# An adaptive-condition FFN on one core: the order of the first loads, who fetches the sample numbers, and how many warm-up matmuls precede the first product

## The reference, cut to what matters

```python
def reference(x, itok, weights, inter_w, inter_b, output_w, output_b):
    # x (32, 64, 1024), itok (32,) with values 0..15, weights (16, 64, 64)
    W = weights[itok]                              # one 64x64 matrix per sample
    y = einsum('bct,bcd->bdt', x, W)               # condition product
    h = gelu(einsum('bsd,df->bsf', y, inter_w) + inter_b)   # 1024 -> 4096
    out = einsum('bsf,fd->bsd', h, output_w) + output_b     # 4096 -> 1024
    return x + out
```

## Time and profile before

| | |
|---|---|
| median of 3 runs | 1261.03 us (1260.89 to 1261.08) |
| profiled execution: own time | 1260.64 us |
| its span | 1258.8 us |
| PE busy | 1253.7 us, 100% of the span |
| DVE busy | 825.6 us, 66% |
| ACT busy | 566.9 us, 45% |
| POOL busy | 188.1 us, 15% |
| granted TensorE clock | 1.0 (mean of the core) |

### The profile page before, as it was taken

The page is one execution under the profiler, slowest core; times in us unless marked ns, Lnnn a source line. Parts: engine busy times, 40 slices in busy tenths (PEclk is TensorE's granted clock), DMA queues, the critical chain, the costliest instruction groups (busy, mean ns, idle before and its releaser), DMA issues.

```text
span 1258.8 us, 15370 instructions
## 1 busy us (share of the span) xinstructions
PE 1253.7 (100%) x5664; PEld 1043.1 (83%) x5664; DVE 825.6 (66%) x1087; ACT 566.9 (45%) x969; POOL 188.1 (15%) x95
## 2 busy tenths in 40 slices
PE   9999999999999999999999999999999999999998
PEld 9888888888888888888888888888888888888887
DVE  5977787676577777657655455554547767784764
ACT  4845454454544444444434444444444444444442
POOL 4362223321000000000034233312200000000000
PEclk9999999999999999999999999999999999999999
DMA  9586655764997322349835224544189932223431
GB/s 343 160 275 244 242 196 222 283 250 177 384 392 283 97 89 99 101 165 360 310 137 195 95 119 174 184 184 145 74 330 396 351 132 93 101 101 100 155 131 51
DMA packets 94090, 249.28 MB, mean 198 GB/s; under 512 B 7328, under 2 KB 15552, under 8 KB 92608
## 3 DMA queue, kind: packets, MB, share of 16 engines
q1 hardware_dynamic: 93408, 248.14, 54.6%
q10 hardware_dynamic: 576, 0.15, 0.1%
q0 software_dynamic: 32, 0.00, 0.0%
HBM read 162.28 MB, written 85.98 MB: 197 GB/s over the span
## 4 chain that ended last, share of the span: by engine, by line
PE 97%; DVE 1%; DMA 1%; SPq 0%; POOL 0%; ACT 0%; issue 0%; ACTq 0%; DVEq 0%
PE ps L580 48%; PE ps L564 48%; DMA w_raw<-in_L_ffn_inter_w_dram 1%; PE ps L517 1%; POOL s_w L476 0%; SPq L321 0%; DVE y_whole L795 0%; DVE acc L878 0%; DVE lhs L800 0%; DVE y_whole L782 0%; DVE y L789 0%; SPq L318 0%; ACT lhs L646 0%; ACT y_stage L623 0%; SPq L317 0%
## 5 line engine op out<-in xcount | busy, mean ns | idle before, releaser
L564 PE MATMUL ps<-y,lhs 128*128 128x512 f32 x2688 | 611.4, 389 | 0.0
L580 PE MATMUL ps<-rhs,lhs 128*128 128x512 f32 x2688 | 609.6, 389 | 0.0
L580 PEld LDWEIGHTS ps<-rhs,lhs 128*128 128x128 f32 x2688 | 504.7, 188 | 104.6
L564 PEld LDWEIGHTS ps<-y,lhs 128*128 128x128 f32 x2688 | 504.2, 188 | 104.3
L716 ACT ACTIVATE lhs<-h_raw 128x512 fp32r<-128x512 f32 x224 | 141.6, 632 | 345.8 <-PE ps L580 340.2
L859 DVE TENSOR_TENSOR lhs<-h_raw,lhs 128x512 fp32r<-128x512 f32 x224 | 155.0, 692 | 188.5 <-ACT lhs L716 188.5
L800 DVE TENSOR_TENSOR lhs<-w_raw,lhs 128x512 fp32r<-128x512 f32 x128 | 111.1, 870 | 131.6 <-ACT lhs L646 131.5
L646 ACT ACTIVATE lhs<-w_raw 128x512 fp32r<-128x512 f32 x128 | 80.9, 633 | 171.7 <-PE ps L564 165.2
L862 DVE TENSOR_TENSOR rhs<-W,rhs 128x512 fp32r<-128x512 f32 x224 | 153.3, 684 | 0.0
L800 DVE TENSOR_TENSOR lhs<-s_w,lhs 128x512 fp32r<-128x512 f32 x96 | 91.3, 953 | 89.3 <-ACT lhs L646 89.1
L468 POOL TENSOR_TENSOR s_w<-w_raw 128x1024 f32<-128x1024 f32 x16 | 48.9, 3055 | 620.3 <-PE ps L580 354.0
(11 more groups left out here) (38 smaller groups left out, 290.1 us busy)
## 6 DMA issues: line engine op xcount, KB each, us to landing
h_raw<-h_mem SPq DMA_DIRECT2D x112, 512.0 KB, 3.3
w_raw<-in_L_ffn_inter_w_dram SPq DMA_DIRECT2D x32, 1024.0 KB, 8.6
h_mem<-hs SPq DMA_DIRECT2D x64, 512.0 KB, 4.5
W<-in_L_ffn_output_w_dram SPq DMA_DIRECT2D x32, 1024.0 KB, 12.4
h_mem<-c SPq DMA_DIRECT2D x48, 512.0 KB, 5.4
y_mem<-y_out SPq DMA_DIRECT2D x28, 512.0 KB, 3.5
y<-y_mem SPq DMA_DIRECT2D x7, 2048.0 KB, 12.8
acc<-in_x_dram SPq DMA_DIRECT2D x16, 512.0 KB, 9.0
```

What stands on the lines that cost most here:

```text
L564: last = nc.tensor.matmul(ps[:, bank, :], w[:, k, :], y[i][:, part, k, :], start=(i in FRESH and k == 0 and u == 0), stop=(k == KH - 1 and ...
L580: last = nc.tensor.matmul(ps[:, bank2(h, j, tb), :], lhs[s % RING][:, a, blk(tb)], rhs[r][:, w, :], start=(j in FRESH and q == 0 and u == ...
```

## The change

- SyncE: the first half of the first token tile goes ahead of the first half of the condition matrices.
- The sample numbers are loaded by ScalarE's queue, ahead of its half of the condition matrices, instead of by GpSimd's; the bias rows by GpSimd's queue instead of ScalarE's.
- Each picking engine reads its first number (`which`) after the wait for the numbers and ahead of the wait for the condition matrices.
- GpSimd makes `ident` behind its six picks; one zeroing of `wdiag` goes to VectorE; the activation that loads the Gelu table reads `ones` and waits for these.
- WARM is 9 instead of 15.

```diff
-    WARM = 15
+    WARM = 9
@@
-        def pick(engine, i):
+        def which(engine, i):
+
+            return engine.value_load(itok_sb[0:1, i:i + 1], min_val=0, max_val=SETS - 1)
+
+        def pick(i, number):
 
             j, s = divmod(i, PER)
-            which = engine.value_load(itok_sb[0:1, i:i + 1], min_val=0, max_val=SETS - 1)
             rows = slice(s * C, (s + 1) * C)
-            return wdiag[rows, j:j + 1, rows], cond_all[:, bass.ds(which, 1), :]
+            return wdiag[rows, j:j + 1, rows], cond_all[:, bass.ds(number, 1), :]
@@ SyncE
+            sp.dma_start(x0[:, 0, 0:BANK], x_tok[0, :, 0, 0:BANK]).then_inc(x0_half, 16)
             sp.dma_start(cond_all[:, 0:SETS // 2], cond_sets[:, 0:SETS // 2]).then_inc(cond_in, 16)
-            sp.dma_start(x0[:, 0, 0:BANK], x_tok[0, :, 0, 0:BANK]).then_inc(x0_half, 16)
             sp.dma_start(x0[:, 0, BANK:D], x_tok[0, :, 0, BANK:D]).then_inc(x0_in[0], 16)
@@ GpSimd
-            pool.dma_start(itok_sb[0:1], itok.rearrange("(o b) -> o b", o=1)).then_inc(itok_in, 16)
+            pool.dma_start(b1_rows[0:F // P], b1.rearrange("(a p) -> a p", p=P)).then_inc(b1_in, 16)
             nc.gpsimd.memset(wdiag[0:C, :, C:P], 0.0).then_inc(wdiag_zero, 1)
-            nc.gpsimd.memset(wdiag[C:P, :, 0:C], 0.0).then_inc(wdiag_zero, 1)
+            pool.wait_ge(itok_in, 16)
+            number = which(pool, 0)
+            pool.wait_ge(cond_in, 32)
+            for i in range(0, TILES * PER, 3):
+                to, of = pick(i, which(pool, i) if i > 0 else number)
+                nc.gpsimd.tensor_copy(to, of).then_inc(picked[0], 1)
             nc.gpsimd.memset(ident[0:F // P], 0.0).then_inc(ident_zero, 1)
...
-            pool.wait_ge(itok_in, 16)
-            pool.wait_ge(cond_in, 32)
-            for i in range(0, TILES * PER, 3):
-                to, of = pick(pool, i)
-                nc.gpsimd.tensor_copy(to, of).then_inc(picked[0], 1)
@@ ScalarE
+            act.dma_start(itok_sb[0:1], itok.rearrange("(o b) -> o b", o=1)).then_inc(itok_in, 16)
             act.dma_start(cond_all[:, SETS // 2:SETS], cond_sets[:, SETS // 2:SETS]).then_inc(cond_in, 16)
-            act.dma_start(b1_rows[0:F // P], b1.rearrange("(a p) -> a p", p=P)).then_inc(b1_in, 16)
-            act.wait_ge(ident_made, 1)
-            nc.scalar.activation(table_ahead[0:F // P, 0:1], ident[0:F // P, 0:1], ACT.Gelu_apprx_tanh)
+            act.wait_ge(ones_made, 1)
+            nc.scalar.activation(table_ahead[:, 0:1], ones[:, 0:1], ACT.Gelu_apprx_tanh)
             act.wait_ge(itok_in, 16)
+            number = which(act, 1)
             act.wait_ge(cond_in, 32)
@@ VectorE
             nc.vector.memset(ones[:], 1.0).then_inc(ones_made, 1)
+            nc.vector.memset(wdiag[C:P, :, 0:C], 0.0).then_inc(wdiag_zero, 1)
             dve.wait_ge(itok_in, 16)
+            number = which(dve, 2)
             dve.wait_ge(cond_in, 32)
```

More of the change, by code:

```diff
@@ L447, in picks1 @@
                 for i in range((TILES + first_j) * PER, (TILES + end_j) * PER):
-                    to, of = pick(pool, i)
+                    to, of = pick(i, which(pool, i))
                     nc.gpsimd.tensor_copy(to, of).then_inc(picked1, 1)
@@ L735, in y1_high @@
                 nc.scalar.activation(y1_out[item % 2][:, 0, :], y1_in[:, (0, 0, 0, 3, 1, 2, 2)[i], :], ACT.Copy).then_inc(y1_hi, 1)
+            act.dma_start(itok_sb[0:1], itok.rearrange("(o b) -> o b", o=1)).then_inc(itok_in, 16)
             act.dma_start(cond_all[:, SETS // 2:SETS], cond_sets[:, SETS // 2:SETS]).then_inc(cond_in, 16)
-            act.dma_start(b1_rows[0:F // P], b1.rearrange("(a p) -> a p", p=P)).then_inc(b1_in, 16)
-            act.wait_ge(ident_made, 1)
-            nc.scalar.activation(table_ahead[0:F // P, 0:1], ident[0:F // P, 0:1], ACT.Gelu_apprx_tanh)
+            act.wait_ge(ones_made, 1)
+            nc.scalar.activation(table_ahead[:, 0:1], ones[:, 0:1], ACT.Gelu_apprx_tanh)
             act.wait_ge(itok_in, 16)
+            number = which(act, 1)
             act.wait_ge(cond_in, 32)
             for i in range(1, TILES * PER, 3):
-                to, of = pick(act, i)
+                to, of = pick(i, which(act, i) if i > 1 else number)
                 nc.scalar.activation(to, of, ACT.Copy).then_inc(picked[1], 1)
@@ L908, in _ @@
             nc.vector.memset(ones[:], 1.0).then_inc(ones_made, 1)
+            nc.vector.memset(wdiag[C:P, :, 0:C], 0.0).then_inc(wdiag_zero, 1)
             dve.wait_ge(itok_in, 16)
+            number = which(dve, 2)
             dve.wait_ge(cond_in, 32)
             for i in range(2, TILES * PER, 3):
-                to, of = pick(dve, i)
+                to, of = pick(i, which(dve, i) if i > 2 else number)
                 nc.vector.tensor_copy(to, of).then_inc(picked[2], 1)
```

## The result

The changed kernel takes 1264.04 us, the median of 18 runs (1261.08 to 1266.40), against 1260.95 (18 runs, 1260.22 to 1262.41) of the kernel before: a ratio of 1.0024, 95% interval 1.0018 to 1.0030. It is 3.1 us slower, and its runs spread over 5.3 us instead of 2.2. The forecast was 1260.9 with a range up to 1262.3; the result lies outside it.

A forecast was written before the change was run, and what follows sets the result against it. TensorE's unbroken matmul run was taken to bound the kernel, its start set by a chain from the first weight DMA. 1261.03 with 0 for the products, -0.1 for that DMA and 0 for the rest gave 1260.9 us, range 1260.3 to 1262.3.

The forecast's parts named there:

- part 1: Start of the condition products: condition matrices there at 5.4 us, first product at about 6.15 instead of 6.55, 0.4 earlier.
- part 5: Six fewer warm-up matmuls at the front: 1.37 us less warm-up but no saving; TensorE idle about 1.15 us, clock term 0.
- rival (d): Front: condition matrices land at 6.5, products start at 7.25; TensorE 0.7 us later, 0.41 free: +0.3, 1261.3 us; chance 6%.
- the skill's ring order: Load queues: SyncE's condition half stands behind the half tile's bytes, landing nearer 6.5 than 4.6; first product no earlier.
- Part 2: Condition products at tile 1: TensorE waits for it until 8.35 us, so of 0.4 us gained 0.03 stay.
- Part 3: End of the products: covered 1.5 us by VectorE's low parts; TensorE's lateness costs nothing for its first 0.41 us.
- Part 4: First weight DMA: issued at 7.24 us again, landing moved by -0.1 us, between -0.41 and +0.2; the term that decides.
- Rival (b): TensorE's clock low for one 3.2 us stretch of the products: 1.6 us lost, 0.41 free, +1.2, 1262.2 us; chance 18%.
- Rival (c): TensorE's clock low for two such stretches, 6.4 us of the products: +2.8, 1263.8 us; chance 3%.
- Part 6: Front, remaining moves (bias rows, `ident`, zeroing, table activation, numbers' load): all covered, cost 0.

The follow-up runs named there:

- hold_tiles: The changed kernel with 15 warm-up matmuls and SyncE waiting for both condition halves ahead of tile 0's second half and everything behind it; 1263.01 us (ratio 1.0015).
- after_w15: The changed kernel with 15 warm-up matmuls instead of 9; 1262.83 us (ratio 1.0015 to the kernel before).
- both_moves: The kernel before with half tile ahead of SyncE's condition half, numbers ahead of ScalarE's, bias rows on GpSimd's queue; 15 warm-up matmuls; 1262.37 us (ratio 1.0009).
- after_w24: The changed kernel with 24 warm-up matmuls instead of 9; 1262.42 us (ratio 1.0008 to the kernel before).
- before_w9: The kernel before with 9 warm-up matmuls instead of 15, nothing else; 1261.58 us (ratio 1.0006).
- early_only: The changed kernel with all loads on the queues and in the order of the kernel before, and 15 warm-up matmuls; 1261.28 us (ratio 0.9999).
- fifteen_narrow: The kernel before with its 15 warm-up matmuls 32 columns wide instead of 128; 1263.49 us (ratio 1.0018).
- before_w25: The kernel before with 25 warm-up matmuls instead of 15; 1262.03 us (ratio 1.0007).
- best: The changed kernel with 15 warm-up matmuls, ScalarE's condition half ahead of the numbers, and the first weight half issued ahead of the last tile; 1260.78 us (ratio 0.9998).
- nine_wide: The kernel before with 9 warm-up matmuls instead of 15, the first six twice as wide (256 columns); 1261.77 us (ratio 1.0003).

## Why the prediction was wrong, point by point

Two terms failed: the landing of the condition matrices (part 1, bound 6.5, measured 8.24) and the clock term of part 5, put at 0.

**Part 1, the start of the products: wrong, and this is the first step that failed.** The half tile landed at 3.5 (said: 3.8 to 5.7), the reads were early, from landing to pick it took 0.12 us (8.24 to 8.36) where I had 0.41. But ScalarE's condition half landed at 8.24, where I had 5.4 and an upper bound of 6.5. The bound was the 4.9 us of the half tile, a load of twice the bytes on the other queue; I took the slowest row near it as the worst case and priced each queue by itself. The rows that bore on it were the later tiles, not the earlier loads: hold_tiles gives 4.0 without them, the changed kernel 6.9 with them. (The upper bound of 7.35 for the first product is also mis-added: 6.5 and the same steps give 7.25, which is what rival (d) uses.) That the condition matrices come later was seen, as rival (d), with 6% and 0.7 us of late start; it was 2.3. I had weighed the skill's ring order, and it was not ring order: the half behind the half tile, SyncE's, landed at 5.1, and the late half was the one of the queue that had next to nothing else in it.

**Part 2, tile 1 gives it back:** never came into play. Tile 1 landed at 2.63 + 5.8 = 8.4, as worked out (8.35).

**Part 3, the cover:** the mechanism was right, its size was off. Of 2.16 us of late products in after_w15 (23.34 against 21.18) 1.47 were left at the long piece, so 0.69 were covered; in the changed kernel it is 3.75 less 2.96, 0.79. The gap is only a part of this. Without a gap the `cond1` behind it is shorter as well:

```profile
40.02 3.57 PE ps L520 x32
```

3.57 us in the changed kernel against the 3.81 at 36.79. I read 0.41 us of slack from the gap alone, whose preceding matmuls have modelled ends.

**Part 4, the weight block:** 6.18 + 12.7 = 18.9 instead of 19.34, within its bounds, but issued 1.06 earlier and not at the same time. In this order of loads it was not last in the chain. The times of the issues vary from execution to execution and with the order (0.38 us for the half tile here, 0.87 before), so they are no constants to be summed.

**Part 5, nine matmuls:** right that the saving is nothing, wrong that the clock term is 0, and this is the second step that failed, by the medians the larger one. They ended at 5.39, not 5.0, since in this execution the clock had not risen in them. Rival (b) had the mechanism and price (1.2 us of 1.6, measured 1.5 in the products) and 18%. The chance was that of a short gap. With the late matrices the gap is 3.48 us, and (b) and (d) become one case: I priced the two as alternatives where one brings on the other. In both_moves and after_w24 the late start costs 1.2 us in the median, in after_w15 1.7; what nine add to it is the rest, 1.9 by the differences to the kernel before on the same chip (3.1 less 1.2). The two go together: nine alone cost 0.4 (before_w9), late matrices alone 1.2 to 1.7, and both 3.1. Rival (c), two stretches of low clock, gave 1263.8 and so nearly the time, for another reason.

**Part 6:** right; early_only stands at 0.0.

The clock that is listed with each run bears part 5 out beyond the one trace. It is 0.998 or less in 8 of the 18 runs of the changed kernel and in 1 of the 176 runs of the experiments (after_w15's 1266.04). A 0.999 says less, since in before_w9 it comes from the end of the run, behind the last matmul.

**What was not in the prediction at all:** that anything between the front and the end could move. In the profiled execution 2.04 us are lost between 67 and 347 us. About 1.0 is lost behind the store of y. The other 1.0 stands at 72.56, where the chain names nothing that TensorE waits for. The timelines name it. The changed kernel, and the kernel before:

```profile
63.75 2.48 POOL L471 TENSOR_TENSOR s_w<-w_raw 128x1024 f32<-128x1024 f32 x1 [15.90 <-issue]
63.91 6.74 DVE L793 TENSOR_TENSOR y<-y_whole,y 128x1024 fp32r<-128x1024 f32 x2
71.17 2.28 DVE L804 TENSOR_TENSOR lhs<-w_raw,lhs 128x512 fp32r<-128x512 f32 x1
73.56 1.62 PE L567 MATMUL ps<-y,lhs 128*128 128x512 f32 x6 [1.00 <-issue]
```

```profile
60.95 2.35 DVE L789 TENSOR_TENSOR y<-y_whole,y 128x1024 fp32r<-128x1024 f32 x2
62.95 2.60 POOL L468 TENSOR_TENSOR s_w<-w_raw 128x1024 f32<-128x1024 f32 x1 [16.85 <-issue]
```

VectorE's pair of `y_low` takes 6.74 us instead of 2.35, because GpSimd's sum of weights started 0.16 us ahead of it, and not 2.0 us behind. Behind it VectorE's next low part of the weights ends at 73.45 (66.10 in the kernel before); `first` waits for that low part (`lhs_lo`), and TensorE starts again at 73.56. All 18 traces agree. In two, this one and fifteen_narrow, GpSimd's sum starts ahead of the pair, the pair takes 6.7 us, and TensorE stands still for 1.0 us until 0.1 us after the low part ends. In two (after_w24, before_w25) it starts 1.03 and 1.04 us behind the pair's start, and the pair takes 4.5. In the other 14 it starts 1.11 us or more behind, and the pair takes 2.35; where it comes closest, GpSimd's sum is the slow one (3.49 us in best, 3.43 in nine_wide, against 2.4). So of these instructions the one that starts first goes on at its own speed, and the other waits. A late front moves the two against each other. How often that happens in executions without a profile is open, as it is for the store of y.

The losses of the median can be told this far: 1.2 us or more from the late condition matrices, and about 1.9 from having nine warm-up matmuls and not 24 with them. The low clock at the front is 1.5 in the profile; the store of y, the meeting of GpSimd and VectorE and the last stores are the rest, and their shares in the median are not separable.

## What to carry to other kernels

A load in small pieces that everything waits for (256 bytes a piece here) should be on its way before the large ones start on any queue: price it by what will share the DMA engines with it until it lands, not by the same load's time in another order. Two moves that are each free can be dear together, so test the pair. Count warm-up matmuls by many executions and not by the profiled one: nine brought 15 of 18 runs above 1263 where fifteen brought 3 of 11. That they should last until the first real product is suggested by 24 (none of 11) and not shown. Look at the upper end of the single runs, but do not read it as a lost clock: of the executions above 1263 us that have a trace, two owed more to stores that an instruction packet fell among than to the front. And follow a late start to the end of the chain, since it also changes which of two engines comes first where they disturb each other.

## What the runs showed of the hardware that I had not expected

- In the trace of fifteen_narrow TensorE ran its 30 warm-up instructions one behind the other from 1.21 to about 7.6 us with all weight loads at 286 to 333 ns, and was at the lower level until 11 us; in the kernel before the weight loads took 192 ns from 4.6 us on. That a warm-up is long did not mean that the clock was up.
- The granted clock of the windows reads 1.00 at the front where the weight loads take 333 ns (before_w9 and fifteen_narrow; the changed kernel shows 0.50 only from 8 us on). The weight loads' duration is the firmer sign.
- One instruction packet of 0.02 MB inside a store of 512 KB went with 1.4 us more until its landing (5.3 against 3.9 us), in 3 of 18 traces, 160 us behind the change; one among the last stores went with 2.0 to 2.1 us more until the end (4.6 and 4.7 us behind the last addition against 2.5 to 2.6), in 2 of 18 traces.
- A subtraction of 128x1024 on VectorE took 3.4 us instead of 1.2 where a sum of 128x1024 on GpSimd had started 0.05 to 0.16 us ahead of it; the other way round GpSimd's took 3.4 to 3.5 us instead of 2.4.
- The four cells of two load orders gave 3.8, 4.2, 3.6 and 6.8 us for the same 128 KB (6.0 to 6.9 in the four traces of the last cell's order).
